# The attention product of a two-layer graph kernel as three reduced-precision passes, moved behind both projections, with the lists of three engines re-ordered

## The chip, the cores and the metric

The kernel runs on one core of a Trainium2 chip. The metric is the device time of one execution in microseconds (us), lower is better.

## The reference

64 graphs of 128 nodes with 256 features pass two attention layers; each adds its result to its input and normalises the row. Cut to what matters:

```python
# layer 0: one score per node, softmax over the nodes
q, k = split(x @ Wqk);  v = x @ Wv
w = (1/16) * mask * sum_d(q * (adj @ (k * mask)))
x = layernorm(x + softmax(w, nodes) * v)
# layer 1: edge-weighted attention without a softmax maximum
query, keyt, value = x @ Wq.T + bq, x @ Wk.T + bk, x @ Wv.T + bv
weight = adj * exp(query @ keyt.T);  weight /= weight.sum(-1)
x = layernorm(x + weight @ value)
```

All inputs and outputs are float32.

## The kernel before

The 64 graphs go through in 32 pairs. `FIRST` is -2 and `DRAIN` is 29: `slots` writes out a list of instructions for each engine per slot `t`, by hand, first unrolled, then as a hardware loop of four slots from t = 4 to 27, then unrolled again, and `drain()` ends it. In slot `t` the engines work on several pairs at once: layer 0 of pairs t+2 to t+4, the transposition, queries, values and scores of layer 1 for pair t, and the attention product and residual of pair t-1. Each engine works its list strictly in order; semaphores (`wait_ge`, `then_inc`) tie the lists together. The names below are those of the code.

Precision: most float32 products are made as three passes over operands split into a high part (a copy rounded to `float32r`) and a low part (the exact remainder). `split_half` (lines 788 to 791) issues hi*hi, hi*lo and lo*hi. Three products are still plain float32: `scores`, the transposes, and `attend` (line 896), which multiplies the edge weights `edge` with `val`. A column of ones in `val` (column `DIM`) makes the row sums for the denominator in the same product.

TensorE's list in a slot (line 944): `aggregate(t+2)`, `project(t+2)` of graph 0, `attend` of pair t-1 for both graphs, `project(t+2)` of graph 1, `queries(t)`, `transpose_w` (line 843), `values(t)`, `scores(t)`, `transpose_p` (line 849), `transpose_next`. 

VectorE's list in a slot (line 682): `sum_x1` (lines 585 and 590), the `edge` product (line 693), `split_x1t` (lines 578 and 580, which make `x1t_hi` and `x1t_lo` for `queries` and `values`), the statistics of layer 0 (line 571), `neg_mean` and `var_eps` (lines 710 and 711), `weight` of graph 0 (line 565), the residual of pair t-1 (lines 724 and 730), `weight` of graph 1, the statistics of layer 1, `neg_max` (line 742), `inv_sum` and `p_row` (lines 750 and 754), `score_bias` (line 616).

GpSimd's list (line 345): `low_x` (line 342), `rstd` as a power of -0.5 (line 355), `shift` (line 358), `mask_adj` (line 274), `xt_lo` (line 365), `x1b` (line 282), `low_adjm` (line 337).

ScalarE's list (line 483): the exponentials `exp_s` (line 438), the copies `x1t` (line 493) and `agg` (line 499), `xt_hi` (line 413), the two normalisations (line 431, two instructions each), `z` (line 444), the exponential of the softmax row (line 527), `adjm_hi` (line 426), `val` (line 542), `x_hi` (line 420).

SyncE issues the loads and stores (lines 219 to 238); they wait on `x1_sum_done`, `edge_done`, `xt_lo_done` and `out_done`.

Of the kernel before, what the change touches and what calls it, by code (L numbers as in the profile page):

```python
# [5 lines left out]
F32 = mybir.dt.float32  # L6
# [27 lines left out]
def build(nc, x_pairs, xt_pairs, adjt_pairs, params0, params1, value_bias, out_pairs):  # L34
    ctx = ExitStack()
    with ctx:
# [57 lines left out]
        score_bias = sb("score_bias", [128, 2])  # L94
        exp_s = sb("exp_s", [128, PAIR_N])
        edge = sb("edge", [128, PAIR_N])
        den_inv = sb("den_inv", [128, 2])


# [54 lines left out]
        score_bias_done, edge_done, den_inv_done = sem("score_bias_done"), sem("edge_done"), sem("den_inv_done")  # L154
        x2_done, stats2_done, stats_cleared, var_eps_done = sem("x2_done"), sem("stats2_done"), sem("stats_cleared"), sem("var_eps_done")
        first_xt_lo_done = sem("first_xt_lo_done")
        x_hi_done, x_lo_done, adjm_hi_done, adjm_lo_done = sem("x_hi_done"), sem("x_lo_done"), sem("adjm_hi_done"), sem("adjm_lo_done")

        xt_lo_done, adjm_done, x1b_done = sem("xt_lo_done"), sem("adjm_done"), sem("x1b_done")
# [107 lines left out]
        def _(pool):  # L267
# [75 lines left out]
                                        x_hi[r % 2][:, :].bitcast(F32), ALU.subtract).then_inc(x_lo_done, 1)  # L343

            def slot(t, r):
                if exists(t + 3) and r + 3 >= SPLIT:
                    low_x(t + 3, r + 3)
                if exists(t + 1) or exists(t - 2):

                    pool.wait_ge(var_eps_done, norms(t))  # L350
                    if exists(t - 1):
                        pool.wait_ge(x1_done, t)
                    if exists(t - 4):
                        pool.wait_ge(out_done, t - 3)
                    nc.gpsimd.tensor_tensor(rstd[r % 2][:, :, :], var_eps[:, :, :], minus_half[:, :, :], ALU.pow)\  # L355
                        .then_inc(rstd_done, 1)
                    pool.wait_ge(rstd_done, norms(t))
                    nc.gpsimd.tensor_tensor(shift[r % 2][:, :, :], neg_mean[:, :, :], rstd[r % 2][:, :, :], ALU.mult)\  # L358
                        .then_inc(shift_done, 1)
                if exists(t + 3) and r + 3 >= SPLIT:  # L360
                    mask_adj(t + 3, r + 3)
                if exists(t + 3):

                    pool.wait_ge(xt_hi_done, t + 4)
                    nc.gpsimd.tensor_tensor(  # L365
                        xt_lo[(r + 3) % 2][:, :, :, :].rearrange("p t g n -> p (t g n)"), xt_raw[(r + 3) % 2][:, :],
                        xt_hi[(r + 3) % 2][:, :, :, :].rearrange("p t g n -> p (t g n)").bitcast(F32), ALU.subtract)\
                        .then_inc(xt_lo_done, 1)
                if r == -2:
                    mask_adj(1, 1)  # L370
                    mask_adj(2, 2)
                    pool.wait_ge(wv1_hi_done, 1)
                    nc.gpsimd.tensor_tensor(wv1_lo[:, :, 0:DIM], wv1T, wv1_hi[:, :, 0:DIM].bitcast(F32), ALU.subtract)\
                        .then_inc(wv1_lo_done, 1)
                if r == -1:
                    mask_adj(3, 3)
                    pool.wait_ge(x1t_lo_done, 1)
                if exists(t + 1):

                    pool.wait_ge(x1_done, t + 2)  # L380
                    if r + 1 == 0:
                        pool.wait_ge(bv_loaded, 16)
                    if exists(t - 1):
                        pool.wait_ge(x2_done, t)
                    add_value_bias(r + 1)
                if exists(t + 3) and r + 3 >= SPLIT:
                    low_adjm(t + 3, r + 3)

            nc.gpsimd.memset(p_row[:, :], 0.0).then_inc(p_row_zeroed, 1)
            nc.gpsimd.memset(ident[:, :], 0.0).then_inc(ident_zeroed, 1)  # L390
            nc.gpsimd.memset(minus_half[:, :, :], -0.5)
            nc.gpsimd.memset(wv1_hi[:, :, DIM:VAL_COLS].bitcast(F32), 0.0)
            nc.gpsimd.memset(wv1_lo[:, :, DIM:VAL_COLS].bitcast(F32), 0.0)
            for v in (val, val_a):
                nc.gpsimd.memset(v[:, :, DIM:DIM + 1], 1.0)
                last = nc.gpsimd.memset(v[:, :, DIM + 1:VAL_COLS], 0.0)
# [10 lines left out]
        def _(act):  # L407
# [75 lines left out]
            def slot(t, r):  # L483
# [7 lines left out]
                if exists(t):  # L491
                    act.wait_ge(x1t_done, t + 1)
                    nc.scalar.copy(x1t[:, :, :, :], x1t_ps).then_inc(x1t_copied, 1)
                if exists(t + 2):

                    act.wait_ge(agg_done, t + 3)
                    if exists(t + 1):
                        act.wait_ge(w_done[1], t + 2)
                    nc.scalar.copy(agg[:, :, :], agg_ps).then_inc(agg_copied, 1)
# [15 lines left out]
                if exists(t + 1):  # L515

                    act.wait_ge(shift_done, norms(t))
                    if exists(t - 1):
                        act.wait_ge(x1b_done, t)
                    norm(x1[(r + 1) % 2], x1_sum[(r + 1) % 2], 0, r, x1_done)  # L520
                if exists(t) and r != 0:
                    act.wait_ge(z_done, t + 1)
                    bias_z(z)
                if exists(t + 2):
# [1 line left out]
                    act.wait_ge(row_max_done, t + 3)  # L526
                    nc.scalar.activation(exp_row_ps(r + 2), w_row_ps(r + 2), ACT.Exp, bias=neg_max[:, 0:1],
                                         accum_out=exp_sum[:, 0:1]).then_inc(row_exp_done, 1)
                if exists(t + 3) and r + 3 >= SPLIT:
                    split_adjm(t + 3, r + 3)  # L530
                if r == DRAIN:
                    act.wait_ge(x1t_done, t + 2)
                    nc.scalar.copy(x1t_a[:, :, :, :], x1t_drain_ps).then_inc(x1t_copied, 1)
# [5 lines left out]
                    nc.scalar.copy(at_hi[:, :, :], at_ps[:, :, 0:DIM]).then_inc(at_hi_done, 1)  # L539
                if exists(t):  # L540
                    act.wait_ge(val_done, t + 1)
                    nc.scalar.copy(val[:, :, 0:DIM], val_ps[:, :, 0:DIM]).then_inc(val_copied, 1)
                if exists(t + 4) and r + 4 >= SPLIT:
                    split_x(t + 4, r + 4)

# [12 lines left out]
        def _(dve):  # L558
# [60 lines left out]
            def drain():  # L619
                a, b = PAIRS - 2, PAIRS - 1  # L620
                n = norms(DRAIN)
                sum_x1(b, b)
                bias_scores(DRAIN)
                for g in range(2):
# [57 lines left out]
            def slot(t, r):  # L682
# [5 lines left out]
                if exists(t - 1):  # L688

                    dve.wait_ge(score_exp_done, t)  # L690
                    if exists(t - 2):
                        dve.wait_ge(sum_done, t - 1)
                    nc.vector.tensor_tensor(edge[:, :], exp_s[:, :], adjt[(r - 1) % 4][:, 0:PAIR_N], ALU.mult)\
                        .then_inc(edge_done, 1)
                if exists(t) and r != 0:
                    split_x1t(t)
                if exists(t + 1):

                    for g in range(2):
# [2 lines left out]
                if exists(t + 1) or exists(t - 2):  # L702

                    if exists(t + 1):
                        dve.wait_ge(stats1_done, t + 2)
                    if exists(t - 2):
                        dve.wait_ge(stats2_done, t - 1)
                    if exists(t) or exists(t - 2):
                        dve.wait_ge(shift_done, norms(t) - 1)
                    nc.vector.tensor_scalar(neg_mean[:, :, :], stats[:, :, :, 1], -1.0, None, ALU.mult)  # L710
                    nc.vector.tensor_scalar(var_eps[:, :, :], stats[:, :, :, 2], 1.0 / DIM, EPS, ALU.mult, ALU.add)\  # L711
                        .then_inc(var_eps_done, 1)
                if r == -1:

                    dve.wait_ge(at_hi_done, 1)
                    nc.vector.tensor_tensor(wv1_lo[:, :, DIM], at_ps[:, :, DIM], wv1_hi[:, :, DIM].bitcast(F32), ALU.subtract)
                    nc.vector.tensor_tensor(at_lo[:, :, :], at_ps[:, :, 0:DIM], at_hi[:, :, :].bitcast(F32), ALU.subtract)\
                        .then_inc(at_lo_done, 1)
                if exists(t + 2):
                    weight(t + 2, r + 2, 0)  # L720
                if exists(t - 1):

                    dve.wait_ge(sum_done, t)
# [8 lines left out]
                            in1=x1b[(r - 1) % 2][:, graph(g)], op0=ALU.mult, op1=ALU.add)  # L732
                    last.then_inc(x2_done, 1)
                if exists(t + 2):
                    weight(t + 2, r + 2, 1)
                if exists(t - 1):
                    dve.wait_ge(x2_done, t)
                    both_stats(1, x2[(r - 1) % 4]).then_inc(stats2_done, 1)
                if exists(t + 2):

                    dve.wait_ge(w_row_done, t + 3)
                    nc.vector.tensor_reduce(neg_max[:, :], w_row_ps(r + 2), AX.X, ALU.max, negate=True).then_inc(row_max_done, 1)
                if r == -1:
                    dve.wait_ge(bias_done, 1)
                    nc.vector.tensor_copy(z_bias[:, :], bias_ps[:, 0:HALVES])
                    nc.vector.tensor_copy(s_bias[:, :], bias_ps[:, HALVES:HALVES + 1]).then_inc(biases_ready, 1)
                if exists(t + 2):

                    dve.wait_ge(row_exp_done, t + 3)
# [37 lines left out]
        def _(pe):  # L787
# [156 lines left out]
            def slot(t, r):  # L944
                if exists(t + 2):
                    if r > 0:
                        aggregate(t + 2, r + 2)
                    project(t + 2, r + 2, 0)
                if exists(t - 1):

                    pe.wait_ge(edge_done, t)
                    pe.wait_ge(val_copied, t)
                    attend(sum_ps, edge, val, 0)
                    attend(sum_ps, edge, val, 1).then_inc(sum_done, 1)
                if exists(t + 2):
                    project(t + 2, r + 2, 1)
                if exists(t):

                    pe.wait_ge(x1t_lo_done, t + 1)
# [97 lines left out]
```

## Time and profile before

| what | value |
|---|---|
| time, median of 3 runs | 305.21 us (304.97 to 305.28) |
| profiled execution: its own time | 305.32 us |
| profiled execution: span | 303.5 us |
| TensorE busy | 293.9 us (97%) |
| VectorE, ScalarE, GpSimd busy | 227.3 us (75%), 215.0 us (71%), 198.2 us (65%) |
| mean granted TensorE clock | 0.994 of full speed |
| HBM traffic | 31.1 MB, 102 GB/s over the span |

The span runs from the first to the last instruction of the program; the time of the same execution is 1.8 us longer and holds what lies around it. Busy time of an engine is a sum over stages; which engine sets the pace of a slot is read from the waits and from the order of time inside one slot.

### The profile page before, as it was taken

To read this page: it belongs to the slowest core of one execution; us is meant where nothing else is said; L and a number is where in the kernel's file an instruction comes from. 1 tells how busy PE (TensorE), PEld (TensorE's weight loads), DVE (VectorE), ACT (ScalarE), POOL (GpSimd) and SP (SyncE) were. 2 spreads that over 40 slices of the span, in tenths; PEclk is the share of its full clock that TensorE was granted. 3 is DMA by queue.
4 is the path that set the end of the run, shared out by engine and by line. 5 is a ranking of instruction groups with operands and counts; after the bars stand their busy time and mean duration, and the time that the engine had idled before them with its cause. 6 is when DMAs were issued, how large, how long until landed. Compare 5 with 4: busy or idle time off the path is not lost.

```text
span 303.5 us, 6829 instructions
## 1 busy us (share of the span) xinstructions
PE 293.9 (97%) x1956; PEld 269.4 (89%) x1956; DVE 227.3 (75%) x691; ACT 215.0 (71%) x509; POOL 198.2 (65%) x237
## 2 busy tenths in 40 slices
PE   8999999999999999999999999999999999999981
PEld 7788999999999999999999999999999999999980
DVE  1476778877777887777788777778877777888583
ACT  3447667778877777887777788777778877776762
POOL 1547766666886666688666667866666787664540
PEclk9999999999999999999999999999999999999997
DMA  7921233332334332224334222434422234210102
GB/s 230 339 73 36 88 89 122 97 107 62 105 121 121 121 113 92 70 89 121 121 121 121 80 73 89 121 121 121 121 89 72 83 119 121 87 54 36 37 35 104
DMA packets 19165, 31.26 MB, mean 103 GB/s; under 512 B 2128, under 2 KB 6608, under 8 KB 19152
## 3 DMA queue, kind: packets, MB, share of 16 engines
q1 hardware_dynamic: 19152, 31.11, 32.6%
q8 instruction: 6, 0.10, 0.1%
q14 instruction: 7, 0.06, 0.1%
HBM read 22.71 MB, written 8.39 MB: 102 GB/s over the span
## 4 chain that ended last, share of the span: by engine, by line
PE 91%; DVE 4%; issue 2%; ACT 1%; POOL 1%; POOLq 0%; DVEq 0%
PE ps L789 22%; PE ps L791 21%; PE ps L790 21%; PE ps L897 8%; PE ps L892 8%; PE ps L874 4%; PE ps L996 1%; PE ps L812 1%; PE ps L849 1%; PE ps L843 1%; DVE stats L571 1%; PE ps L1001 1%; DVE x L609 1%; PE ps L854 1%; POOL x1t_lo_a L303 0%
## 5 line engine op out<-in xcount | busy, mean ns | idle before, releaser
L355 POOL TENSOR_TENSOR rstd<-var_eps,minus_half 128x4 f32<-128x4 f32 x31 | 31.6, 1018 | 72.4 <-DVE var_eps L711 72.4
L431 ACT ACTIVATE x<-x_sum,shift,rstd 128x256 f32<-128x256 f32 x62 | 33.9, 595 | 59.7 <-POOL shift L358 59.6
L789 PE MATMUL ps<-w_hi,xt_hi 128*128 128x512 f32 x128 | 56.8, 444 | 0.5 <-DVE w_lo L775 0.5
L791 PE MATMUL ps<-w_hi,xt_lo 128*128 128x512 f32 x128 | 50.3, 393 | 0.0
L790 PE MATMUL ps<-w_lo,xt_hi 128*128 128x512 f32 x128 | 50.3, 393 | 0.0
L282 POOL TENSOR_TENSOR x1b<-x,bv_all 128x512 f32<-128x512 f32 x32 | 41.3, 1290 | 6.7 <-DVE x L609 3.5
L365 POOL TENSOR_TENSOR xt_lo<-xt_raw,xt_hi 128x512 fp32r<-128x512 f32 x31 | 39.8, 1285 | 3.0 <-ACT xt_hi L413 3.0
L342 POOL TENSOR_TENSOR x_lo<-x_raw,x_hi 128x512 fp32r<-128x512 f32 x28 | 36.1, 1290 | 3.4 <-ACT x_hi L420 2.1
L789 PE MATMUL ps<-wv_hi,x1t_hi 128*128 128x258 f32 x124 | 37.9, 305 | 0.0
L791 PE MATMUL ps<-wv_hi,x1t_lo 128*128 128x258 f32 x124 | 35.3, 285 | 0.0
L790 PE MATMUL ps<-wv_lo,x1t_hi 128*128 128x258 f32 x124 | 35.1, 283 | 0.0
L790 PE MATMUL ps<-x1t_lo,at_hi 128*128 128x256 f32 x124 | 35.1, 283 | 0.0
L791 PE MATMUL ps<-x1t_hi,at_lo 128*128 128x256 f32 x124 | 34.9, 282 | 0.0
L789 PE MATMUL ps<-x1t_hi,at_hi 128*128 128x256 f32 x124 | 34.9, 281 | 0.0
L431 ACT ACTIVATE x<-x,shift,rstd 128x256 f32<-128x256 f32 x62 | 33.7, 595 | 0.0
L897 PE MATMUL ps<-val,edge 128*128 128x258 f32 x124 | 32.1, 381 | 1.3 <-DVE edge L596 1.3
L892 PE MATMUL ps<-x1t,z 128*128 128x128 f32 x248 | 32.7, 275 | 0.0
L565 DVE CUSTOM_DVE_ANT_0 agg<-ps,agg,adjt 128x256 f32<-128x256 f32 x64 | 30.5, 480 | 1.0 <-PE ps L791 1.0
L590 DVE SCALAR_TENSOR_TENSOR x_sum<-ps,p_col,x_raw 128x256 f32<-128x256 f32 x64 | 28.0, 479 | 3.2
L892 PEld LDWEIGHTS ps<-x1t,z 128*128 128x128 f32 x248 | 30.4, 191 | 0.0
L444 ACT ACTIVATE z<-ps,z_bias 128x256 f32<-128x256 f32 x62 | 26.0, 470 | 4.0 <-PE ps L791 3.6
L791 PEld LDWEIGHTS ps<-w_hi,xt_lo 128*128 128x128 f32 x128 | 24.0, 188 | 5.3
(128 smaller groups left out, 787.9 us busy)
## 6 DMA issues: line engine op xcount, KB each, us to landing
xt_raw<-xt_pairs SPq DMA_DIRECT2D x32, 256.0 KB, 2.8
x_raw<-x_pairs SPq DMA_DIRECT2D x32, 256.0 KB, 3.1
out_pairs<-x SPq DMA_DIRECT2D x31, 256.0 KB, 2.5
adjt<-adjt_pairs SPq DMA_DIRECT2D x32, 129.0 KB, 2.0
p<-params SPq DMA_DIRECT2D x1, 770.0 KB, 7.1
p<-params SPq DMA_DIRECT2D x1, 512.0 KB, 3.8
p<-params SPq DMA_DIRECT2D x1, 256.0 KB, 4.9
out_pairs<-x SPq DMA_DIRECT2D x2, 128.0 KB, 1.8
```

Source lines behind the costliest of these rows:

```text
L282: nc.gpsimd.tensor_tensor(x1b[r % 2][:, :].rearrange("p (g d) -> p g d", g=2), x1[r % 2][:, :].rearrange("p (g d) -> p g d", g=2), bv_all[ ...
L342: nc.gpsimd.tensor_tensor(x_lo[r % 2][:, :], x_raw[r % 4][:, :], x_hi[r % 2][:, :].bitcast(F32), ALU.subtract).then_inc(x_lo_done, 1)
L355: nc.gpsimd.tensor_tensor(rstd[r % 2][:, :, :], var_eps[:, :, :], minus_half[:, :, :], ALU.pow)\
L365: nc.gpsimd.tensor_tensor(xt_lo[(r + 3) % 2][:, :, :, :].rearrange("p t g n -> p (t g n)"), xt_raw[(r + 3) % 2][:, :], xt_hi[(r + 3) % 2][ ...
L431: last = nc.scalar.activation(out[:, graph(g)], in_[:, graph(g)], ACT.Identity, bias=shift[r % 2][:, layer, g:g + 1], scale=rstd[r % 2][:, ...
L565: nc.vector.tensor_tensor_reduce(agg[:, g, :], y_ps(r)[:, g, :], agg[:, g, :], adjt[r % 4][:, PAIR_N + g:PAIR_N + g + 1], 0.0, ALU.mult, A ...
L590: nc.vector.scalar_tensor_tensor(out=x1_sum[r % 2][:, graph(g)], in0=v0_ps(r)[:, g, :], scalar=p_col[:, g:g + 1], in1=x_raw[r % 4][:, grap ...
L789: nc.tensor.matmul(out, s_hi, m_hi, start=first, stop=False)
L790: nc.tensor.matmul(out, s_hi, m_lo, start=False, stop=False)
L791: return nc.tensor.matmul(out, s_lo, m_hi, start=False, stop=last)
L892: mm = nc.tensor.matmul(out[:, g, :], zs[:, k, graph(g, NODES)], xs[:, k, g, :], start=(k == 0), stop=(k == HALVES - 1))
L897: return nc.tensor.matmul(out[:, g, 0:VAL_COLS], edges[:, graph(g, NODES)], vals[:, g, :], start=True, stop=True)
```

## The change

Four new tiles are added: `edge_hi`, `edge_lo`, `val_hi`, `val_lo`. In the slots the attention product is no longer one float32 matmul per graph but `split_product` over them, and it is issued after both projections, not between them. (The last three pairs, in `drain()`, keep the float32 `attend`.) To feed it, ScalarE copies `edge` into `edge_hi`, GpSimd computes `edge_lo`, ScalarE writes the value copy into `val_hi` in place of `val`, and VectorE computes `val_lo`. The lists are re-ordered:

- GpSimd: `edge_lo` first, which waits for `edge_hi`; `low_x` moves from the head of the list to behind `shift`; `low_adjm` moves ahead of `x1b`.
- ScalarE: `edge_hi` behind the copy of `x1t`; `split_adjm` moves from behind the softmax exponential to ahead of `z`.
- VectorE: behind `edge` now come the statistics of layer 0, `neg_mean`, `var_eps`, then `val_lo`, then `split_x1t`; both `weight` calls stand together; `neg_max` is taken before the statistics of layer 1.

```diff
 # GpSimd
             def slot(t, r):
-                if exists(t + 3) and r + 3 >= SPLIT:
-                    low_x(t + 3, r + 3)
+                if exists(t - 1):
+                    pool.wait_ge(edge_hi_done, t)
+                    nc.gpsimd.tensor_tensor(edge_lo[:, :], edge[:, :], edge_hi[:, :].bitcast(F32), ALU.subtract)\
+                        .then_inc(edge_lo_done, 1)
...
                 if exists(t + 3) and r + 3 >= SPLIT:
+                    low_x(t + 3, r + 3)
                     mask_adj(t + 3, r + 3)
...
+                if exists(t + 3) and r + 3 >= SPLIT:
+                    low_adjm(t + 3, r + 3)
...
-                if exists(t + 3) and r + 3 >= SPLIT:
-                    low_adjm(t + 3, r + 3)
...
 # ScalarE
+                if exists(t - 1):
+
+                    act.wait_ge(edge_done, t)
+                    if exists(t - 2):
+                        act.wait_ge(sum_done, t - 1)
+                    nc.scalar.copy(edge_hi[:, :], edge[:, :]).then_inc(edge_hi_done, 1)
...
+                if exists(t + 3) and r + 3 >= SPLIT:
+                    split_adjm(t + 3, r + 3)
                 if exists(t) and r != 0:
                     act.wait_ge(z_done, t + 1)
                     bias_z(z)
...
-                if exists(t + 3) and r + 3 >= SPLIT:
-                    split_adjm(t + 3, r + 3)
...
-                    nc.scalar.copy(val[:, :, 0:DIM], val_ps[:, :, 0:DIM]).then_inc(val_copied, 1)
+                    to = val if r == DRAIN else val_hi
+                    nc.scalar.copy(to[:, :, 0:DIM], val_ps[:, :, 0:DIM]).then_inc(val_copied, 1)
...
 # VectorE
                     if exists(t - 2):
-                        dve.wait_ge(sum_done, t - 1)
+                        dve.wait_ge(edge_lo_done, t - 1)
                     nc.vector.tensor_tensor(edge[:, :], exp_s[:, :], adjt[(r - 1) % 4][:, 0:PAIR_N], ALU.mult)\
                         .then_inc(edge_done, 1)
-                if exists(t) and r != 0:
-                    split_x1t(t)
...
+                if exists(t - 1):
+
+                    dve.wait_ge(val_copied, t)
+                    nc.vector.tensor_tensor(val_lo[:, :, 0:DIM], val_ps[:, :, 0:DIM], val_hi[:, :, 0:DIM].bitcast(F32),
+                                            ALU.subtract).then_inc(val_lo_done, 1)
+                if exists(t) and r != 0:
+                    split_x1t(t)
...
                 if exists(t + 2):
-                    weight(t + 2, r + 2, 0)
+                    for g in range(2):
+                        weight(t + 2, r + 2, g)
...
 # TensorE
                     project(t + 2, r + 2, 0)
-                if exists(t - 1):
-
-                    pe.wait_ge(edge_done, t)
-                    pe.wait_ge(val_copied, t)
-                    attend(sum_ps, edge, val, 0)
-                    attend(sum_ps, edge, val, 1).then_inc(sum_done, 1)
                 if exists(t + 2):
                     project(t + 2, r + 2, 1)
+                if exists(t - 1):
+
+                    pe.wait_ge(edge_lo_done, t)
+                    pe.wait_ge(val_lo_done, t)
+                    for g in range(2):
+                        n = graph(g, NODES)
+                        mm = split_product(sum_ps[:, g, 0:VAL_COLS], [(edge_hi[:, n], edge_lo[:, n],
+                                                                       val_hi[:, g, :], val_lo[:, g, :])])
+                    mm.then_inc(sum_done, 1)
```

## Rows read from the trace of the kernel before

**Rows 1.** One slot: length; busy us (count) of PE, PEld, DVE, ACT, POOL; clock.

```profile
142.88:151.69 8.81, 8.81 (x64) 8.16 (x61) 7.00 (x21) 6.70 (x17) 6.26 (x7) 1.00 0.34 104
```

**Rows 2.** TensorE in order of time, that slot: start, duration (us), line, operation.

```profile
142.40 0.27 PE L849 MATMUL ps<-ident,p_row 128*128 128x128 f32 x1
...
147.34 0.28 PE L789 MATMUL ps<-x1t_hi,at_hi 128*128 128x256 f32 x1
```

**Rows 3.** The chain that ended last, 140 to 160 us: start, time it holds.

```profile
145.25 0.87 PE ps L897 x4
...
149.64 0.12 PE ps L791
```

**Rows 4.** Line 693, all executions: count, duration ns min/median/max, first and last start.

```profile
L693 DVE TENSOR_TENSOR edge<-exp_s,adjt x29: 414/695/706, 29.0 to 276.1; 128x256 f32<-128x256 f32 x29
```

**Rows 5.** VectorE in order of time, same slot.

```profile
143.76 0.71 DVE L693 TENSOR_TENSOR edge<-exp_s,adjt 128x256 f32<-128x256 f32 x1
...
144.84 0.69 DVE L580 TENSOR_TENSOR x1t_lo<-x1t,x1t_hi 128x512 fp32r<-128x512 f32 x1
145.45 0.70 DVE L571 BATCH_NORM_STATS2 stats<-x_sum 128x6 f32<-128x512 f32 x1
146.18 0.17 DVE L710 TENSOR_SCALAR neg_mean<-stats 128x4 f32<-128x4 f32 x1
146.26 0.16 DVE L711 TENSOR_SCALAR var_eps<-stats 128x4 f32<-128x4 f32 x1
```

**Rows 6.** GpSimd in order of time, same slot; in brackets idle before.

```profile
142.89 1.29 POOL L342 TENSOR_TENSOR x_lo<-x_raw,x_hi 128x512 fp32r<-128x512 f32 x1
146.58 1.02 POOL L355 TENSOR_TENSOR rstd<-var_eps,minus_half 128x4 f32<-128x4 f32 x1 [2.40 <-DVE var_eps L711]
147.68 0.20 POOL L358 TENSOR_TENSOR shift<-neg_mean,rstd 128x4 f32<-128x4 f32 x1
147.83 0.61 POOL L274 TENSOR_TENSOR adjm<-adjt 128x256 f32<-128x256 f32 x1
```

**Rows 7.** Slot 29 in order of time; GpSimd has no `low_x` there.

```profile
276.12 0.41 DVE L693 TENSOR_TENSOR edge<-exp_s,adjt 128x256 f32<-128x256 f32 x1
...
276.46 0.42 DVE L578 CAST x1t_hi<-x1t 128x512 fp32r<-128x512 f32 x1
```

**Rows 8.** The drain in order of time, VectorE and GpSimd side by side.

```profile
291.25 1.33 POOL L282 TENSOR_TENSOR x1b<-x,bv_all 128x512 f32<-128x512 f32 x1 [3.54 <-DVE x L609]
...
292.10 0.52 DVE L599 TENSOR_SCALAR neg_mean<-stats 128x2 f32<-128x2 f32 x1
...
292.53 0.15 DVE L600 TENSOR_SCALAR var_eps<-stats 128x2 f32<-128x2 f32 x1
...
295.72 0.20 POOL L294 TENSOR_TENSOR shift<-neg_mean,rstd 128x2 f32<-128x2 f32 x1
295.73 0.46 DVE L596 TENSOR_TENSOR edge<-exp_s,adjt 128x256 f32<-128x256 f32 x1 [0.74 <-ACT exp_s L438]
```

**Rows 9.** Set-up in order of time: VectorE first, GpSimd behind it.

```profile
7.37 0.75 DVE L775 TENSOR_TENSOR w_lo<-p,w_hi 128x256 fp32r<-128x256 f32 x2
...
7.72 0.87 POOL L274 TENSOR_TENSOR adjm<-adjt 128x256 f32<-128x256 f32 x1 [6.08 <-DMA adjt<-adjt_pairs]
```

**Rows 10.** By line, all executions: durations of operations like the new ones (ns).

```profile
L717 DVE TENSOR_TENSOR at_lo<-ps,at_hi x1: 679/679/679, 16.9 to 16.9; 128x512 fp32r<-128x512 f32 x1
...
L337 POOL TENSOR_TENSOR adjm_lo<-adjm,adjm_hi x28: 718/735/752, 35.9 to 274.4; 128x256 fp32r<-128x256 f32 x28
...
L426 ACT CAST adjm_hi<-adjm x28: 388/388/389, 35.3 to 273.6; 128x256 fp32r<-128x256 f32 x28
```

**Rows 11.** The drain: a TensorE start that came from a wait.

```profile
283.54 1.27 POOL L303 TENSOR_TENSOR x1t_lo_a<-x1t_a,x1t_hi_a 128x512 fp32r<-128x512 f32 x1 [1.18 <-ACT x1t_hi_a L534]
...
284.87 0.39 PE L789 MATMUL ps<-x1t_hi_a,at_hi 128*128 128x256 f32 x1 [0.45 <-POOL x1t_lo_a L303]
```

**Rows 12.** ScalarE in order of time, same slot.

```profile
148.97 0.84 ACT L444 ACTIVATE z<-ps,z_bias 128x256 f32<-128x256 f32 x2
```

More of the change, by code:

```diff
@@ L96, in build @@
         edge = sb("edge", [128, PAIR_N])
+        edge_hi = sb("edge_hi", [128, PAIR_N], F32R)
+        edge_lo = sb("edge_lo", [128, PAIR_N], F32R)
+        val_hi = sb("val_hi", [128, 2, VAL_COLS], F32R)
+        val_lo = sb("val_lo", [128, 2, VAL_COLS], F32R)
         den_inv = sb("den_inv", [128, 2])
@@ L156, in build @@
         first_xt_lo_done = sem("first_xt_lo_done")
+        edge_hi_done, edge_lo_done, val_lo_done = sem("edge_hi_done"), sem("edge_lo_done"), sem("val_lo_done")
         x_hi_done, x_lo_done, adjm_hi_done, adjm_lo_done = sem("x_hi_done"), sem("x_lo_done"), sem("adjm_hi_done"), sem("adjm_lo_done")
@@ L393, in _ @@
             nc.gpsimd.memset(wv1_lo[:, :, DIM:VAL_COLS].bitcast(F32), 0.0)
+            nc.gpsimd.memset(val_hi[:, :, DIM:DIM + 1].bitcast(F32), 1.0)
+            nc.gpsimd.memset(val_hi[:, :, DIM + 1:VAL_COLS].bitcast(F32), 0.0)
+            nc.gpsimd.memset(val_lo[:, :, DIM:VAL_COLS].bitcast(F32), 0.0)
             for v in (val, val_a):
@@ L621, in drain @@
                 n = norms(DRAIN)
+                dve.wait_ge(edge_lo_done, DRAIN)
                 sum_x1(b, b)
@@ L734, in slot @@
                 if exists(t + 2):
-                    weight(t + 2, r + 2, 1)
-                if exists(t - 1):
-                    dve.wait_ge(x2_done, t)
-                    both_stats(1, x2[(r - 1) % 4]).then_inc(stats2_done, 1)
-                if exists(t + 2):
                     dve.wait_ge(w_row_done, t + 3)
@@ L746, in slot @@
                     nc.vector.tensor_copy(s_bias[:, :], bias_ps[:, HALVES:HALVES + 1]).then_inc(biases_ready, 1)
+                if exists(t - 1):
+                    dve.wait_ge(x2_done, t)
+                    both_stats(1, x2[(r - 1) % 4]).then_inc(stats2_done, 1)
                 if exists(t + 2):
@@ L948, in slot @@
                     project(t + 2, r + 2, 0)
-                if exists(t - 1):
-                    pe.wait_ge(edge_done, t)
-                    pe.wait_ge(val_copied, t)
-                    attend(sum_ps, edge, val, 0)
-                    attend(sum_ps, edge, val, 1).then_inc(sum_done, 1)
                 if exists(t + 2):
                     project(t + 2, r + 2, 1)
+                if exists(t - 1):
+                    pe.wait_ge(edge_lo_done, t)
[5 more added lines that the diff above has]
+                    mm.then_inc(sum_done, 1)
                 if exists(t):
```

## The prediction

> **What bounds the kernel now.** I read the windows view of one slot first. TensorE is busy for the whole 8.81 us of it, at full clock, while VectorE has 7.00, ScalarE 6.70 and GpSimd 6.26 us of work [rows 1]. In the waits view TensorE waits for nobody between 30 and 275 us. So a slot is as long as TensorE's list, and time taken out of that list comes off the total until some other chain through the slot is as long. The period is (276.1 - 29.0) / 28 = 8.82 us [rows 4], and 29 slots hold an attention product (x29).
>
> Two more views tell how near the other chains are. The order of time on VectorE and GpSimd shows that `edge`, `x1t_hi` and `x1t_lo` now run at 143.76 to 145.53, and that GpSimd is idle from 144.18 to 146.58, waiting for `var_eps` [rows 5, 6]. Those three VectorE operations have almost no GpSimd beside them. The exception is `edge`, and it shows what company costs: it takes 0.41 us where GpSimd is idle [rows 7] and 0.70 us in the median [rows 4]. In the slot shown `low_x` ends at 142.89 + 1.29 = 144.18 and `edge` at 144.47, 0.29 us later: `edge` was held until the GpSimd operation had ended, then ran its last 0.28 to 0.29 us.
>
> Three more rows say how far this goes. In the drain `neg_mean`, a 0.17 us operation [rows 5], took 0.52 us beside a GpSimd operation that ended at 292.58: it ended at 292.62, and `var_eps` at 292.68, 0.10 us behind it [rows 8]. There too `edge` started 0.01 us behind a `shift` of only 0.20 us that ended at 295.92; it ended at 296.19, again 0.27 to 0.28 us behind it, so even an operation on two columns held it to its own end [rows 8]. In the other order, `mask_adj` took 0.87 us for its usual 0.61 [rows 6, 9] when two VectorE operations ran until 8.12: it ended at 8.59, VectorE's end plus its own duration less 0.14 us. So for each of the two the second comer is held until the first has ended.
>
> The Trainium skill states this as a rule ("SBUF — State Buffer", section "Who interferes with whom"): VectorE and GpSimd share a pair of SBUF ports under an exclusive lock held for the whole instruction, which a VectorE instruction wants if it has two SBUF inputs or runs a two-port mode, as a float32 copy or `tensor_scalar` in SBUF can. By that rule `edge`, `x1t_hi`, `x1t_lo`, `neg_mean` and `var_eps` want the lock and `val_lo`, which reads PSUM, doesn't; the rows agree for `edge` and `neg_mean`, and no row shows `x1t_hi` or `x1t_lo` beside GpSimd. It speaks against this change, which puts the four of them beside GpSimd's work.
>
> **TensorE's own part.** Removed per slot: four float32 passes that hold the chain for 0.87 us. Added: six passes of 258 columns at the 0.12 us of a pass in `values` [rows 3], 0.72 us. Gain 0.15 us a slot. With nothing else late the period would be 8.67 us.
>
> **The new chain in a slot.** Times are counted from the start of `transpose_p` (T = 142.40 [rows 2]). From it hang `p_col`, `x1_sum` and then `edge`, which starts at T + 1.36 [rows 5]; these do not change.
> - `edge`: `low_x` has left its place, GpSimd is free there, so 0.41 us, end 1.77. This is a gain of 0.29 us.
> - Statistics of layer 0 start 0.34 us after `edge` (the step behind it in [rows 7]): 1.70. `neg_mean` would start 0.73 us later [rows 5]: 2.43.
> - `edge_hi` on ScalarE: it waits for `edge`. Behind a wait I take 0.06 us (GpSimd's end at 284.81, TensorE's start at 284.87 [rows 11]); 1.83 plus 0.39 us [rows 10] is 2.22.
> - `edge_lo` on GpSimd: 2.28 to 3.02 (0.735 us, as `adjm_lo` [rows 10]). It has begun 0.15 us before `neg_mean` wants to start, so `neg_mean` ends at 3.06 and `var_eps` at 3.12, as in [rows 8].
> - `rstd` on GpSimd follows `var_eps` by 0.16 us (146.42 to 146.58 [rows 5, 6]): 3.28 to 4.30.
> - `val_lo`: 0.68 us (`at_lo`, the same shape out of PSUM [rows 10]), 3.12 to 3.80. A following operation starts 0.08 us before the end (144.84 + 0.69 against 145.45 [rows 5]), so `x1t_hi` wants to start at 3.72, when `rstd` is in the middle.
> - `x1t_hi`: held until 4.30, plus the tail of 0.28 us: 4.58. (It has `edge`'s duration, 0.42 us [rows 7].)
> - `shift` is ready at 4.38 and is held by `x1t_hi`: 4.58 + 0.20 - 0.14 = 4.64. `x1t_lo` is ready at 4.61, held until 4.64, tail 0.28 + (0.69 - 0.41) = 0.56: it ends at 5.20. It was 145.53 - 142.40 = 3.13 before.
> - `queries` on TensorE waits for it: 0.06 us to the weight load and 0.11 us more to the matmul (the first one after that wait ends 0.11 us later than its start plus the 0.28 us of one [rows 2, 11]). Start 5.37; before, 147.34 - 142.40 = 4.94.
> - From `queries` to the next `transpose_p` TensorE needs 8.82 - 4.94 = 3.88 us, as before. Period 9.25 us.
>
> So `x1t_lo`, which had 1.6 us of slack, becomes the last wait in the slot, and the 0.15 us vanish in it. The unmeasured term is how long `rstd` holds VectorE. Bounds: not at all, and to its end. I take its end, by the 0.20 us `shift`, the nearest row.
>
> **What lies beside other work.** `edge_hi` (0.39 us) falls where ScalarE's list has room: 6.70 + 0.39 of 9.25 us [rows 1]. The copies of `agg` and `xt_hi` behind it are used only after 4 us. GpSimd: 6.26 + 0.74 us plus what it is held. `low_x`, now behind `shift`, starts when `x1t_lo` ends: 5.20 + 1.29 - 0.14 = 6.35; `mask_adj` until 6.96; `adjm_hi`, which ScalarE now does ahead of `z`, until 7.4; `z` until 8.25 (0.84 us [rows 12]). `scores` wants `z` some 24 passes of 0.12 us and a transpose behind `queries`, at 8.3 to 8.4, so this chain fits with 0.1 us; if not, it costs up to 0.1 us a slot (3 us), a bound for the top of the range. `xt_lo`, `adjm_lo`, `x1b` (1.29, 0.74 and 1.29 us more) end at T + 10.3, 1.0 us into the next slot, ahead of its `edge`. TensorE's waits for `edge_lo` (3.02) and `val_lo` (3.80) end before it reaches the product at 4.2. The `weight` calls, the residual and `p_row` all come before their readers. SyncE's loads wait on the same events, at most 0.9 us later, with the next use a slot away. The three memsets in set-up (about 0.1 us each) run while GpSimd waits 6.08 us for a transfer [rows 9]: nothing. `drain()` is the same but for a wait that is long over.
>
> **Sum.** 9.25 - 8.82 = 0.43 us a slot, times 29 is 12.5 us. 303.5 + 12.5 = 316.0 us of span; the profiled execution's time was 1.8 us over its span and 0.1 us over the median, so 317.7 us.
>
> **The rivals.**
> - *`rstd` does not hold VectorE; `edge_lo` does hold `neg_mean`.* `x1t_hi` 3.72 to 4.14, `x1t_lo` 4.18 to 4.87, `queries` 5.04, period 8.92: +0.10 x 29 = 2.9 us, 308.1. For it: `rstd` touches four columns and computes most of its 1.02 us. Against: `shift` on two columns held to its end. Chance 0.16.
> - *`rstd` holds, `neg_mean` slips in ahead of `edge_lo`* (0.15 us decide). `rstd` 3.0 to 4.02, `x1t_hi` 4.30, `x1t_lo` 4.92, `queries` 5.09, period 8.97: +4.4 us, 309.6. Chance 0.12.
> - *GpSimd takes `low_x` before the waiting `x1t_lo`.* Then `x1t_lo` comes at 4.6 + 1.29 + 0.56 = 6.45, `queries` 6.62, period 10.50: +1.68 x 29 = 49 us, 354. It is decided by who is served when `shift` ends at 4.64, VectorE being ready at 4.61. Chance 0.08.
> - *Faster: no hold in the new places.* `neg_mean` 2.43, `val_lo` 2.67, `x1t_hi` 3.28, `x1t_lo` 3.73 to 4.42, `queries` could start at 4.59, before TensorE gets there (4.94 - 0.15 = 4.79). Period 8.67, -4.4 us, 300.8. It decides as soon as `x1t_lo` ends before T + 4.77. For it: the list has room on every engine. Against: the rows on `neg_mean` and `edge`. Chance 0.12.
>
> The forecast has 0.52. 306 to 322 holds it with the first two rivals, 0.80. Within 0.2% (0.6 us, what a measurement of this kernel can tell from no change) I give 0.05, out of the first rival and the faster one with a small hold; faster 0.11, slower 0.84. The forecast's own range is 313 to 321.
>
> **What would show it.** In the changed kernel: attention passes 0.12 us apart; `edge` at 0.41 us; `neg_mean` at about 0.6 us instead of 0.17; `x1t_hi` at about 0.86 us, ending 0.28 us behind `rstd`; `x1t_lo` at 0.6 to 0.7; TensorE idle some 0.5 us before `queries` in each slot with `x1t_lo` as releaser; VectorE's waits for ScalarE shorter. It is wrong if `x1t_hi` stays at 0.42 us beside `rstd`, if `x1t_lo` waits for `low_x`, or if TensorE's last wait is for `z` or `p_row`.

## The result, and the profile after

The changed kernel takes 307.48 us (median, 307.11 to 308.0) against 305.09 us before: ratio 1.0076, 95% interval 1.0063 to 1.0088. It is slower by 2.4 us. The forecast was slower by 12.5 us, 317.7 us; the direction held and the size did not. The time lies where the first rival put it (308.1 us).

In the changed kernel's code the lines have moved: 812 to 814 are the three passes, 872 is `transpose_p`, 915 `scores`; VectorE's `edge` is 712, `neg_mean` 727, `var_eps` 728, `val_lo` 733, `x1t_hi` 596, `x1t_lo` 598; GpSimd's `edge_lo` is 353, `rstd` 362, `shift` 365, `low_x` 347, `mask_adj` 279.

One slot by the windows view of the changed kernel, to be set beside [rows 1] (length; busy us and count of PE, PEld, DVE, ACT, POOL; clock, DMA share, GB/s):

```profile
144.28:153.18 8.90, 8.90 (x65) 8.20 (x64) 7.66 (x22) 7.05 (x19) 7.21 (x9) 1.00 0.34 103
```

The slot is 8.90 us long for 8.81, at full clock. TensorE counts as busy throughout, because gaps of 0.1 to 0.2 us disappear in the modelled ends of its matmuls; the chain view shows them below.

TensorE and `transpose_p` in order of time, changed kernel (T = 143.79):

```profile
143.79 0.28 PE L872 MATMUL ps<-ident,p_row 128*128 128x128 f32 x1
...
147.85 0.28 PE L812 MATMUL ps<-val_hi,edge_hi 128*128 128x258 f32 x1
147.97 0.28 PE L813 MATMUL ps<-val_lo,edge_hi 128*128 128x258 f32 x1
...
148.64 0.39 PE L812 MATMUL ps<-x1t_hi,at_hi 128*128 128x256 f32 x1
...
152.69 0.28 PE L872 MATMUL ps<-ident,p_row 128*128 128x128 f32 x1
```

The passes of the product are 0.12 us apart, as forecast. The first pass of `queries` shows 0.39 us where its neighbours show 0.28, the mark of a start that came from a wait (as in [rows 11]).

The chain that ended last, changed kernel, around that pass (start, time it holds):

```profile
148.61 0.12 PE ps L814
148.73 0.30 PE ps L812
149.03 0.12 PE ps L813
```

A pass that should hold the chain for 0.12 us holds it for 0.30: TensorE lost about 0.2 us before `queries`. Over the loop this is the rule: from the end of the product's last pass to the end of the twelve passes of `queries` TensorE takes 1.60 us in the median slot, and 1.41 us in experiment 2, where nothing is late. The waits view puts only 0.9 us of waits for `x1t_lo` down in all, in 6 slots; this loss must be read from the order of time.

VectorE, same slot, to be set beside [rows 5]:

```profile
145.17 0.41 DVE L712 TENSOR_TENSOR edge<-exp_s,adjt 128x256 f32<-128x256 f32 x1
145.50 0.71 DVE L589 BATCH_NORM_STATS2 stats<-x_sum 128x6 f32<-128x512 f32 x1
146.24 0.62 DVE L727 TENSOR_SCALAR neg_mean<-stats 128x4 f32<-128x4 f32 x1
146.78 0.16 DVE L728 TENSOR_SCALAR var_eps<-stats 128x4 f32<-128x4 f32 x1
146.85 0.68 DVE L733 TENSOR_TENSOR val_lo<-ps,val_hi 128x512 fp32r<-128x512 f32 x1
147.45 0.41 DVE L596 CAST x1t_hi<-x1t 128x512 fp32r<-128x512 f32 x1
147.90 0.69 DVE L598 TENSOR_TENSOR x1t_lo<-x1t,x1t_hi 128x512 fp32r<-128x512 f32 x1
```

GpSimd, same slot, beside [rows 6]:

```profile
146.10 0.74 POOL L353 TENSOR_TENSOR edge_lo<-edge,edge_hi 128x256 fp32r<-128x256 f32 x1 [1.35 <-ACT edge_hi L510]
147.10 1.02 POOL L362 TENSOR_TENSOR rstd<-var_eps,minus_half 128x4 f32<-128x4 f32 x1 [0.26 <-DVE var_eps L728]
148.19 0.45 POOL L365 TENSOR_TENSOR shift<-neg_mean,rstd 128x4 f32<-128x4 f32 x1
```

Reading the two together: `edge` has no GpSimd operation beside it, 0.41 us. `neg_mean` is held until `edge_lo` ends at 146.84: 0.62 us for 0.17. `x1t_hi` starts in the middle of `rstd` (147.10 to 148.12) and takes 0.41 us, and `x1t_lo` starts in it too and takes its 0.69: neither is held. It is so in every slot: `x1t_hi` starts inside `rstd` 29 times and takes 0.41 to 0.43 us each time. `shift` is then held by `x1t_lo` until 148.59, 0.45 us for 0.20. So `x1t_lo` ends at T + 4.80, not at T + 5.20.

### The profile page after: what moved, and what is told of

Its sections match the earlier page's. It is cut to its first block, busy times and chain, and to the rows that moved or that the text cites. A ratio compares the mean times of both kernels' runs of the same rounds, so it can differ in the third digit from the quotient of the medians.

```text
span 306.2 us, 7064 instructions
## 1 busy us (share of the span) xinstructions
PE 295.2 (96%) x2014; PEld 270.0 (88%) x2014; DVE 247.9 (81%) x720; ACT 224.7 (73%) x538; POOL 226.8 (74%) x269
## 4 chain that ended last, share of the span: by engine, by line
PE 89%; DVE 3%; issue 2%; DMA 2%; ACT 1%; POOL 1%; SPq 0%; POOLq 0%; DVEq 0%
PE ps L812 25%; PE ps L813 23%; PE ps L814 23%; PE ps L915 9%; PE ps L897 4%; DMA p<-params 2%; PE ps L872 1%; PE ps L835 1%; PE ps L866 1%; DVE stats L589 1%; DVE x L627 1%; PE ps L877 1%; POOL x1t_lo_a L308 0%; POOL rstd L362 0%; ACT x L442 0%
## 5 line engine op out<-in xcount | busy, mean ns | idle before, releaser
L812 PE MATMUL ps<-w_hi,xt_hi 128*128 128x512 f32 x128 | 50.9, 398 | 1.4 <-DVE w_lo L798 1.4
L353 POOL TENSOR_TENSOR edge_lo<-edge,edge_hi 128x256 fp32r<-128x256 f32 x29 | 21.5, 740 | 40.4 <-ACT edge_hi L510 40.4
L812 PE MATMUL ps<-x1t_hi,at_hi 128*128 128x256 f32 x124 | 37.4, 301 | 0.0
L915 PE MATMUL ps<-x1t,z 128*128 128x128 f32 x248 | 34.7, 283 | 0.0
L812 PEld LDWEIGHTS ps<-w_hi,xt_hi 128*128 128x128 f32 x128 | 24.0, 188 | 6.3 <-issue 2.2
L583 DVE CUSTOM_DVE_ANT_0 agg<-ps,agg,adjt 128x256 f32<-128x256 f32 x64 | 28.3, 478 | 1.3 <-PE ps L814 1.3
```

Of the source, the lines that this page charges most:

```text
L353: nc.gpsimd.tensor_tensor(edge_lo[:, :], edge[:, :], edge_hi[:, :].bitcast(F32), ALU.subtract)\
L583: nc.vector.tensor_tensor_reduce(agg[:, g, :], y_ps(r)[:, g, :], agg[:, g, :], adjt[r % 4][:, PAIR_N + g:PAIR_N + g + 1], 0.0, ALU.mult, A ...
L812: nc.tensor.matmul(out, s_hi, m_hi, start=first, stop=False)
L915: mm = nc.tensor.matmul(out[:, g, :], zs[:, k, graph(g, NODES)], xs[:, k, g, :], start=(k == 0), stop=(k == HALVES - 1))
```

## The experiments

The times are medians, each beside runs of the kernel before on the same chip (305.15 us for the first four, 305.07 us for the last four; 305.09 us beside the changed kernel, so times of different experiments can be set side by side to 0.1 us). "Period" is the median distance of two `transpose_p` in the loop, counted from each trace: 8.81 us before, 8.90 in the changed kernel. T is again the start of `transpose_p`. The theories A, B and C are those of the expectations.

**1. `val_lo` ahead of `neg_mean`.** The changed kernel with one exchange in VectorE's list:

```diff
+                if exists(t - 1):
+                    dve.wait_ge(val_copied, t)
+                    nc.vector.tensor_tensor(val_lo...).then_inc(val_lo_done, 1)
                 if exists(t + 1) or exists(t - 2):
                     ... neg_mean, var_eps ...
-                if exists(t - 1):
-                    dve.wait_ge(val_copied, t)
-                    nc.vector.tensor_tensor(val_lo...).then_inc(val_lo_done, 1)
```

> Theory A (the hold of neg_mean by edge_lo, through x1t_lo, sets the 8.90 us period): val_lo now stands ahead of neg_mean, so it runs while edge_lo is on GpSimd; neg_mean is held for under 0.2 us instead of 0.45, x1t_lo ends at about T + 4.25 instead of 4.80, TensorE is the bound again at 8.67 to 8.72 us, time 301 to 302.5 us. Theory B (the lost time comes from adjm_hi standing ahead of z): the z chain gains at most the 0.25 us that shift was held; neg_mean's hold is gone and the time stays at 306 to 307.5 us. Theory C (three passes cost what four did): 305 us, the time before.

Measured: 302.25 us, ratio 0.9900 (0.9884 to 0.9915), period 8.68. Against the changed kernel that is 5.2 us less. `x1t_lo` ends at T + 4.21 (median) and TensorE's gap before `queries` is gone. A smaller one is left before `scores`. ScalarE and TensorE there, first experiment:

```profile
138.46 0.41 ACT L437 CAST adjm_hi<-adjm 128x256 fp32r<-128x256 f32 x1 [0.73 <-POOL adjm L279]
138.77 0.84 ACT L455 ACTIVATE z<-ps,z_bias 128x256 f32<-128x256 f32 x2
```

```profile
139.67 0.48 PE L915 MATMUL ps<-x1t,z 128*128 128x128 f32 x2
```

ScalarE idles 0.73 us for `mask_adj` with the work for `z` behind it in its list; `z` ends at 139.61 and `scores` starts 0.06 us later. This is theory A, with B's mechanism as a close second.

**2. The same, and `adjm_hi` back behind the softmax exponential.**

```diff
-                if exists(t + 3) and r + 3 >= SPLIT:
-                    split_adjm(t + 3, r + 3)
                 if exists(t) and r != 0:
                     act.wait_ge(z_done, t + 1)
                     bias_z(z)
                 ... exponential of the softmax row ...
+                if exists(t + 3) and r + 3 >= SPLIT:
+                    split_adjm(t + 3, r + 3)
```

> The same swap, and adjm_hi back behind the softmax exponential on ScalarE. Theory A: as the swap alone, or up to 0.05 us a slot less if z is still a close second: 300.5 to 302 us. Theory B: this one falls to 301 where the swap alone does not. Theory C: 305 us.

Measured: 299.19 us (298.81 to 299.97), ratio 0.9797 (0.9784 to 0.9810), period 8.60, 1.3 us under the lowest time that I had given to theory A. It beats the kernel before by 6.0 us and the changed one by 8.3. One slot of it, VectorE and GpSimd in order of time (T = 131.75):

```profile
134.08 0.67 DVE L722 TENSOR_TENSOR val_lo<-ps,val_hi 128x512 fp32r<-128x512 f32 x1
134.67 0.15 DVE L732 TENSOR_SCALAR neg_mean<-stats 128x4 f32<-128x4 f32 x1
134.74 0.16 DVE L733 TENSOR_SCALAR var_eps<-stats 128x4 f32<-128x4 f32 x1
134.81 0.41 DVE L596 CAST x1t_hi<-x1t 128x512 fp32r<-128x512 f32 x1
135.25 0.69 DVE L598 TENSOR_TENSOR x1t_lo<-x1t,x1t_hi 128x512 fp32r<-128x512 f32 x1
```

```profile
134.05 0.74 POOL L353 TENSOR_TENSOR edge_lo<-edge,edge_hi 128x256 fp32r<-128x256 f32 x1 [1.00 <-ACT edge_hi L510]
135.05 1.05 POOL L362 TENSOR_TENSOR rstd<-var_eps,minus_half 128x4 f32<-128x4 f32 x1 [0.26 <-DVE var_eps L733]
```

`val_lo` reads PSUM and fills the time in which `edge_lo` runs; `neg_mean` comes 0.1 us before `edge_lo` ends and is not lengthened. In 24 slots counted pass by pass, TensorE loses nothing between the product and the next `transpose_p`: each part of its list there takes the same time in all of them, to 2 ns. The period of 8.60 us is TensorE's list alone, 0.07 us below the 8.67 that I had worked out.

**3. The changed kernel with `adjm_hi` alone put back.** The edit is the second half of experiment 2.

> The changed kernel with only adjm_hi put back behind the softmax exponential. Theory A: the period stays with x1t_lo (4.80 + 0.17 + 3.88 = 8.85 us), so at most 0.05 us a slot comes back, 306 to 307.3 us. Theory B: the whole loss comes back, 301 to 303 us.

Measured: 305.23 us (305.12 to 305.91), ratio 1.0002 (0.9993 to 1.0012), period 8.83. It brings 2.2 us, more than theory A's bound of 1.5 and far from theory B's full return. `neg_mean` still takes 0.62 us, `x1t_lo` still ends at T + 4.79 (median) and the gap before `queries` is still there; what is gone is the gap before `scores` (the eight passes of `scores` hold TensorE for 0.95 us in the changed kernel and for 0.89 here). Third experiment, VectorE:

```profile
135.79 0.62 DVE L727 TENSOR_SCALAR neg_mean<-stats 128x4 f32<-128x4 f32 x1
```

The medians of the periods add up: -0.22 for the exchange, -0.07 for `adjm_hi`, -0.30 for both. The times do so less well (5.2 + 2.2 against 8.3 us).

**4. The changed kernel with the float32 product.** All split operands are made and waited for, but nothing reads them; the product takes `edge` and a float32 copy of the values.

```diff
                     for g in range(2):
-                        n = graph(g, NODES)
-                        mm = split_product(sum_ps[:, g, 0:VAL_COLS], [(edge_hi[:, n], edge_lo[:, n], ...)])
+                        mm = attend(sum_ps, edge, val, g)
```

> The changed kernel, but its product in the slot is the float32 one on edge and the float32 copy of the values; edge_hi, edge_lo and val_lo are still made and waited for, and nothing reads them. TensorE has 0.15 us more work a slot. Theory A: TensorE only waits less for x1t_lo, the time stays within 0.5 us of the changed kernel (307.5). If TensorE's own work were the bound, or if the two products cost the same: 4.4 us more (311.9), or no change with TensorE's wait unchanged.

Measured: 308.26 us (307.8 to 308.44), ratio 1.0093 (1.0078 to 1.0109), period 8.90. Against the changed kernel's 307.48 that is 0.8 us, a little over the 0.5 us expected and far from 4.4. The trace shows where the difference went: in the median slot the product takes TensorE 0.87 us in place of 0.72, and `queries` 1.46 in place of 1.60. What the dearer product costs, the shorter wait for `x1t_lo` gives back, so the cheaper one bought almost nothing in the lists it came with.

**5. The 299.19 us version with the float32 product.** The edit is that of experiment 4 on the kernel of experiment 2.

> The version with val_lo ahead of neg_mean and adjm_hi behind the exponential (299.2 us, TensorE without a gap), but with the float32 product in the slot, on edge and the float32 copy of the values; the split operands are still made and waited for. If TensorE's list alone sets the time there: 0.15 us a slot more for the product (4 passes of 0.218 against 6 of 0.121), 4.4 us, 303 to 304.5 us. If something else holds the time: within 1 us of 299.2.

Measured: 303.65 us, ratio 0.9948 (0.9935 to 0.9961). The product is worth 303.65 - 299.19 = 4.5 us where TensorE alone sets the time; the expected 4.4 was 0.15 us times 29.

**6. Probes of two SBUF columns beside `rstd` and beside `low_x`,** in the kernel before; nothing reads what they write.

```diff
                     ... var_eps ...
+                if exists(t + 2) and exists(t - 1):
+                    for c in range(20):
+                        nc.vector.tensor_tensor(comb[:, 2 * c:2 * c + 2], ident[:, 0:2], ident[:, 2:4], ALU.mult)
...
+                if exists(t + 2) and exists(t - 1):      # ahead of edge
+                    for c in range(6):
+                        nc.vector.tensor_tensor(comb[:, 40 + 2 * c:42 + 2 * c], ident[:, 0:2], ident[:, 2:4], ALU.mult)
```

> The kernel before with probes on VectorE: 20 products of two SBUF columns right behind var_eps, beside rstd and shift, and six of them ahead of edge, beside low_x. Nothing reads their results. Theory of the record (a GpSimd operation holds to its own end): one probe beside rstd lasts until rstd's end, about 1 us. Theory after the result (only the part of the operation that moves data holds; rstd moves four columns and computes for the rest): probes beside rstd run at their own pace of 0.06 to 0.1 us but for at most 0.2 us in all; the first probe beside low_x is held to low_x's end, 0.4 us, in both theories.

Measured: the probes make a slot 1.6 us longer and the kernel takes 350.46 us (one run); only the durations matter. All 20 probes of one slot (ns min/median/max), and in order of time VectorE's probes and GpSimd in another slot:

```profile
L719 DVE TENSOR_TENSOR comb<-ident x20: 147/149/180, 146.4 to 147.8; 128x2 f32<-128x2 f32 x20
```

```profile
167.23 1.56 DVE L719 TENSOR_TENSOR comb<-ident 128x2 f32<-128x2 f32 x20
```

```profile
167.48 1.02 POOL L356 TENSOR_TENSOR rstd<-var_eps,minus_half 128x4 f32<-128x4 f32 x1 [2.83 <-DVE var_eps L715]
168.58 0.20 POOL L359 TENSOR_TENSOR shift<-neg_mean,rstd 128x4 f32<-128x4 f32 x1
```

No probe waited out `rstd`: the longest of all 580 took 193 ns. Counted instruction by instruction, in each of the 29 slots exactly one probe beside `rstd` is lengthened, by 0.03 to 0.05 us. It starts 0.03 to 0.11 us behind `rstd`'s start and ends 0.21 to 0.30 us behind it, and the rest of `rstd`'s 1.02 us passes unnoticed. Beside `shift` (0.20 us) one probe in each slot takes 0.17 to 0.18 us, and it ends 0.01 us behind `shift`'s end. The first probe beside `low_x`, same kernel:

```profile
163.36 1.29 POOL L343 TENSOR_TENSOR x_lo<-x_raw,x_hi 128x512 fp32r<-128x512 f32 x1 [0.71 <-ACT x_hi L421]
...
164.23 0.43 DVE L691 TENSOR_TENSOR comb<-ident 128x2 f32<-128x2 f32 x1
```

It starts at 164.23 and ends with `low_x`, at 164.65; in all 28 slots the first probe ends 0.02 us behind `low_x`. So `low_x` and `shift` hold VectorE to their own ends and `rstd` doesn't: what it holds is over when a `shift` started in its place would be over, 0.8 us before its own end. The theory of the record is wrong. The second one, that an operation holds VectorE only while it moves data, fits all three (`shift` and `rstd` both move four columns), but it isn't shown: no run has a power on many columns, so whether the few columns or the kind of operation makes the hold short stays open.

**7. The 299.19 us version with the product between the projections,** where the float32 one was: `project(t + 2, r + 2, 1)` is issued behind the product.

> The 299.2 us version with the split product issued between the projections, where the float32 one was. TensorE reaches it at T + 2.65 and edge_lo ends at 3.04, so TensorE waits about 0.55 us there, and queries start at 5.32 at the earliest: period 9.15 us, 315 us. If the place did not matter: 299 to 300 us.

Measured: 316.81 us (316.48 to 317.14), ratio 1.0377 (1.0362 to 1.0393), period 9.21. From the waits view, TensorE's weight loads (us in total, times, longest):

```profile
PEld ps L812 <- POOL edge_lo L353: 20.9, 29, 0.7
```

The weight loads wait in all 29 slots, 0.72 us each. They run ahead of the matmuls, so TensorE itself loses less: the six passes of the product hold it for 1.28 us there and for 0.72 in experiment 2, a loss of 0.55 us, as expected. Behind both projections `edge_lo` is off the path; between them the split product costs more than it saves (316.81 us against 305.07).

**8. Which VectorE operations are held.** Three `tensor_reduce` and three `tensor_scalar` on a few SBUF columns ahead of `edge`, beside `low_x`, in the kernel before; nothing reads their results.

```diff
+                if exists(t + 2) and exists(t - 1):
+                    for c in range(3):
+                        nc.vector.tensor_reduce(comb[:, 2 * c:2 * c + 1], ident[:, 0:4], AX.X, ALU.max, negate=True)
+                    for c in range(3, 6):
+                        nc.vector.tensor_scalar(comb[:, 2 * c:2 * c + 2], ident[:, 0:2], -1.0, None, ALU.mult)
```

> The kernel before with three tensor_reduce and three tensor_scalar of two to four SBUF columns on VectorE ahead of edge, beside low_x. Nothing reads their results. If neg_mean was held because a float32 tensor_scalar in SBUF reads through both ports: the reduces run unheld (under 0.2 us each), the first tensor_scalar ends with low_x. If any VectorE operation on SBUF is held: the first reduce is held. If none is: all six run at their own pace.

Measured: 307.32 us (one run), period 8.91. All executions (ns min/median/max), and `low_x` in one slot:

```profile
L691 DVE TENSOR_REDUCE comb<-ident x87: 143/146/150, 28.5 to 277.9; 128x1 f32<-128x4 f32 x87
```

```profile
L693 DVE TENSOR_SCALAR comb<-ident x87: 153/156/282, 28.7 to 278.1; 128x2 f32<-128x2 f32 x87
```

```profile
143.31 1.29 POOL L343 TENSOR_TENSOR x_lo<-x_raw,x_hi 128x512 fp32r<-128x512 f32 x1
```

The reduces run at one pace beside `low_x`; the first `tensor_scalar` behind them is held, by up to 0.13 us; in this slot it is held until 144.63 where `low_x` ends at 144.60, and in 25 of 28 slots it ends 0.02 to 0.03 us behind `low_x` (in the other three it starts too late to be held for long). So the kind of VectorE operation decides as well, and `neg_mean`, held beside `edge_lo`, is a `tensor_scalar`.

## Why the prediction was wrong

By its own steps:

- **TensorE's own part.** The passes of the product are 0.12 us apart, right; the gain of 0.15 us a slot measured as 4.5 us in all (experiment 5), right. The floor of the period was 8.60 and not 8.67, because the rest of TensorE's list did not stay as it was: in experiment 2 `aggregate`, `queries` and `values` take 0.02 to 0.03 us less each than before.
- **`edge`, its followers, `edge_hi`, `edge_lo`.** Forecast T + 1.36, 1.70, 1.83, 2.28; measured 1.38, 1.71, 1.82, 2.31. Right. So was that `edge` would take 0.41 us.
- **`neg_mean` held by `edge_lo`.** Forecast end 3.06; measured 146.86 - 143.79 = 3.07. Right, and experiment 1, which takes this hold away, gives back the larger part of what the lists lose: 5.2 of 8.3 us.
- **`val_lo`.** Forecast end 3.80; measured 3.74, since it starts 0.07 us behind the start of `var_eps` and not at its end. Small.
- **`x1t_hi` held until `rstd` ends.** This is the step that failed, "I take its end, by the 0.20 us `shift`, the nearest row". Forecast: held to 4.30, end 4.58. Measured: not held, 0.41 us, end 147.86 - 143.79 = 4.07. All that follows inherits it: `x1t_lo` 5.20 for 4.80, period 9.25 for 8.90. Of the 10 us by which the forecast is off, 0.35 us a slot times 29 is all.
- **What the row had shown.** In [rows 8] `edge` beside `shift` was 0.04 us longer than alone, and I read that as a hold to the end of the 0.20 us operation. For `shift` this is right: in experiment 6 the probe beside it ends with it. Carried over to `rstd` it is wrong: there the probe is longer by the same 0.03 to 0.05 us, and ends 0.8 us before `rstd` does. A row on an operation of 0.20 us cannot tell "to its end" from "for its first 0.2 us". The bound "not at all" was nearly right, and the chance of 0.16 for it was too low.
- **`adjm_hi` ahead of `z`.** "this chain fits with 0.1 us; if not, it costs up to 0.1 us a slot (3 us)": it did not quite fit, though `shift` came earlier than forecast. Experiment 3 puts it at 0.07 us a slot, 2.2 us.
- **The sum.** 0.21 us gained on TensorE's list (8.60 in place of 8.81), against 0.22 us of `x1t_lo` and 0.07 us of `z`: +0.08 us a slot, 2.3 us over 29 slots; measured 2.4. These terms are read from the runs after the result. The forecast had the first one at 0.15 and the second at 0.58 (0.43 + 0.15).

The rival in which `rstd` does not hold VectorE and `edge_lo` does hold `neg_mean` had `x1t_lo` at 4.87 and the period at 8.92, and the trace has 4.80 and 8.90. That its 308.1 us lie so near 307.48 is in part luck: its `x1t_lo` ended 0.07 us too late, and it had no term for `z`, which costs as much. The rival "`low_x` before the waiting `x1t_lo`" never came up, as `x1t_lo` did not wait. The faster rival's bound, "as soon as `x1t_lo` ends before T + 4.77", agrees with two runs: in experiment 3 `x1t_lo` ends at 4.79 and the time is that of the kernel before, in experiment 1 it ends at 4.21 and the time is 302.25.

The rule of the Trainium skill that the prediction cites ("SBUF — State Buffer", "Who interferes with whom") names the right VectorE operations as far as the runs go: experiment 8 agrees that a `tensor_scalar` is held and a `tensor_reduce` is not, and in experiment 2 `val_lo`, which reads PSUM, runs beside `edge_lo` at its own 0.67 us. That the first comer keeps the ports "for the whole instruction" agrees with `low_x`, `shift` and `edge_lo` and not with `rstd`: there the measurement decides, 0.03 to 0.05 us longer beside an operation of 1.02 us.

Open: every fourth slot, where the hardware loop turns, is longer by 0.03 to 0.4 us, and by differing amounts in these kernels (mean less median of the period: 0.01 us before and after, 0.05 in experiment 1). There TensorE stops once: before a pass of the projections in the kernel before and in experiments 2 and 3, and before the first pass of `aggregate` in the changed kernel and in experiment 1, where the chain view has 0.22 us of "issue" in one such place, a wait for nothing that the profile shows. What it waits for was not tried; it is the likely reason that the times of experiments 1 and 3 do not quite add up.

## What to carry to other kernels

A cheaper instruction on the bounding engine is worth its full price only if the lists that feed it still arrive in time: here a product worth 4.5 us came with lists that lost 8.3 us (the changed kernel against experiment 2) to one 0.45 us hold and one wrong order of two ScalarE operations, and both could be repaired by moving existing lines. In this kernel it paid to put a VectorE operation that reads PSUM beside GpSimd's long SBUF operation, and the small `tensor_scalar` on SBUF, on which the chain hangs, behind it. When one row could be read as "held to the end" and as "held for a moment", because the operation is short, it bounds nothing for a long one: give both ends a like chance, or find a case in which they differ.

## What the runs showed of the hardware that was not expected

- GpSimd's power on 128x4 elements takes 1.02 us and makes one two-input VectorE operation near its start 0.03 to 0.05 us longer, no more than `shift` with its 0.20 us does; a VectorE cast and a two-input subtraction, both of 512 columns, started later in it and ran at 0.41 and 0.69 us, as alone.
- Where GpSimd is the one held, it follows the formula of the prediction (VectorE's end plus its own duration less 0.14 us): in experiment 2 `x1t_hi` ends at 135.22 and `rstd` takes 1.05 us for 1.02; in the changed kernel `shift` is held by `x1t_lo` from 0.20 to 0.45 us, its end 148.64 being `x1t_lo`'s end 148.59 plus 0.20 less 0.14, to 0.01 us.
- TensorE's list is 0.05 us a slot shorter with the float32 product behind both projections than between them (period 8.76 in experiment 5 against 8.81 before), but the product itself holds TensorE for 0.87 us in both places. What gets shorter is mainly `values`, 1.43 us for 1.46, and `aggregate`, 0.71 for 0.73, in the median slot. In experiment 7, with the split product between the projections, `values` takes 1.46 us again. The cause was not tried.
